# Order of work in the choice of experts and in the first rope: a two-layer kernel of attention and experts on one core

## What is computed

```python
x = x + tanh(g_xattn[0]) * xattn0(layernorm(x), ctx, ...)   # 16 heads; queries and context rows with rope
x = x + tanh(g_ffn[0])   * ffn0(layernorm(x), ...)          # 8 experts, top 2
x = x + tanh(g_xattn[1]) * xattn1(layernorm(x), ctx, ...)   # 16 heads; rope on the context alone
x = x + tanh(g_ffn[1])   * ffn1(layernorm(x), ...)          # 16 experts, top 2, and a shared expert
...
# ffn1
logits = xt @ Wr.T + bias
topk_val, topk_idx = top_k(softmax(logits), 2)
w = topk_val / (sum(topk_val) + 1e-9)
y = einsum('tei,eih->teh', silu(xt @ Wg) * (xt @ Wu), Wd)   # only the two chosen experts of a token count
routed = einsum('tke,tk,teh->th', one_hot(topk_idx), w, y)
shared = (silu(xt @ sWg) * (xt @ sWu)) @ sWd
return routed + shared
```

## Time and profile before

| what | value |
|---|---|
| median of 3 runs | 529.0 us (528.54 to 530.12) |
| profiled execution | 532.13 us |
| its span, first to last instruction | 530.3 us |
| PE busy | 469.5 us (89%) |
| DVE busy | 385.2 us (73%) |
| ACT busy | 197.5 us (37%) |
| POOL busy | 172.4 us (33%) |
| mean granted TensorE clock | 0.939 |

### The profile page before, as it was taken

One profiled execution on the slowest core, in us unless ns is written; L12 is line 12 of the kernel. 1 busy time (PEld: TensorE's weight loads), 2 busy tenths in 40 slices (PEclk: granted clock), 3 DMA queues, 4 the chain that ended last, 5 costly groups with the idle time before them and its releaser, 6 DMA issues.

```text
span 530.3 us, 9094 instructions
## 1 busy us (share of the span) xinstructions
PE 469.5 (89%) x3172; PEld 390.8 (74%) x3172; DVE 385.2 (73%) x847; ACT 197.5 (37%) x376; POOL 172.4 (33%) x150
## 2 busy tenths in 40 slices
PE   4699999999999999998999899999999976899700
PEld 4468667667765799887889788887799865899600
DVE  6979889889889865789777848677855585666323
ACT  3224233132151531433332356654662501466400
POOL 4825101101104000364551023532273306564064
PEclk9899999999999899999999999999799777999955
DMA  8302202211420300002100534322312303369344
GB/s 271 119 1 79 80 3 77 79 37 42 138 77 1 136 2 1 0 1 61 37 24 1 202 96 135 105 74 90 119 61 91 100 1 83 95 171 143 110 123 131
DMA packets 20286, 42.42 MB, mean 80 GB/s; under 512 B 3392, under 2 KB 10816, under 8 KB 20256
## 3 DMA queue, kind: packets, MB, share of 16 engines
q1 hardware_dynamic: 18000, 35.85, 20.3%
q0 software_dynamic: 2256, 6.16, 5.7%
HBM read 35.85 MB, written 6.16 MB: 79 GB/s over the span
## 4 chain that ended last, share of the span: by engine, by line
PE 63%; DVE 16%; issue 9%; POOL 6%; DMA 3%; ACT 1%; POOLq 0%; SPq 0%; DVEq 0%
PE ps L581 12%; PE ps L582 12%; PE ps L583 12%; PE ps L733 8%; PE ps L629 3%; POOL fg L564 2%; PE ps L681 2%; PE ps L589 2%; POOL probs L448 2%; PE ps L639 1%; DMA xg<-xn_rows,idx 1%; POOL experts_split L470 1%; PE ps L602 1%; PE ps L996 1%; DVE rstd L1488 1%
## 5 line engine op out<-in xcount | busy, mean ns | idle before, releaser
L448 POOL TENSOR_TENSOR probs<-probs,rowrec 128x512 f32<-128x512 f32 x28 | 28.7, 1045 | 160.3 <-DVE rowrec L1547 160.0
L1103 ACT ACTIVATE PT_hi<-ps 128x512 fp32r<-128x512 f32 (+1 forms) x64 | 35.5, 600 | 55.8 <-PE ps L639 52.4
L581 PE MATMUL ps<-xs_hi,A_hi 128*128 128x512 f32 x128 | 52.4, 409 | 1.5 <-DVE xs_lo L1501 1.5
L583 PE MATMUL ps<-xs_hi,A_lo 128*128 128x512 f32 x128 | 50.5, 395 | 0.0
L582 PE MATMUL ps<-xs_lo,A_hi 128*128 128x512 f32 x128 | 50.4, 394 | 0.0
L1510 DVE TENSOR_TENSOR PT_lo<-ps,PT_hi 128x512 fp32r<-128x512 f32 (+1 forms) x64 | 41.4, 686 | 7.7 <-ACT PT_hi L1103 7.3
L470 POOL TENSOR_TENSOR experts_split<-experts_raw,experts_split 128x768 fp32r<-128x768 f32 (+1 forms) x16 | 29.2, 1843 | 26.6 <-ACT experts_split L1103 26.6
L556 POOL DMA_INDIRECT xg<-xn_rows,idx x31 | 30.1, 970 | 21.2 <-PE ps L996 11.5
L581 PE MATMUL ps<-N_hi,PT_hi 128*128 128x256 f32 x128 | 36.4, 284 | 0.0
L582 PE MATMUL ps<-N_lo,PT_hi 128*128 128x256 f32 x128 | 36.1, 282 | 0.0
L583 PE MATMUL ps<-N_hi,PT_lo 128*128 128x256 f32 x128 | 36.0, 281 | 0.0
(11 more groups left out here) (224 smaller groups left out, 1333.5 us busy)
## 6 DMA issues: line engine op xcount, KB each, us to landing
W<-attn SPq DMA_DIRECT2D x8, 704.0 KB, 4.1
W<-attn SPq DMA_DIRECT2D x8, 672.0 KB, 4.4
W<-attn SPq DMA_DIRECT2D x16, 320.0 KB, 4.3
y_rows<-yout SPq DMA_DIRECT2D x15, 256.0 KB, 3.1
WF<-ffn SPq DMA_DIRECT2D x8, 384.0 KB, 4.2
experts_raw<-ffn SPq DMA_DIRECT2D x2, 1536.0 KB, 6.8
experts_raw<-ffn SPq DMA_DIRECT2D x2, 1152.0 KB, 5.6
X<-x SPq DMA_DIRECT2D x4, 256.0 KB, 4.9
```

Source lines behind the costliest of these rows:

```text
L448: nc.gpsimd.tensor_tensor(part, part, rowrec[:, 4 * h:4 * h + 4, :].unsqueeze(3).to_broadcast([P, 4, 2, L]), ALU.mult).then_inc(s.p, 1)
L581: nc.tensor.matmul(dst, lhs[0], rhs[0], start=start, stop=False)
L583: return nc.tensor.matmul(dst, lhs[1], rhs[0], start=False, stop=stop)
L1103: return nc.scalar.activation(dst, src, ACT.Copy)
```

## The change

- GpSimd's rope waits until VectorE has normalised its last tile of the first norm.
- ScalarE splits all three experts of the last weight group ahead of the transposed tiles of the last norm, instead of one there and two behind.
- In `sparse_ffn` TensorE does the first half's sums between the second router and `ranks`, and the shared expert's second half between `positions` and `slot_tokens`. The bridges change: three ahead of the transposes go, fifteen ahead of `ranks` become five ahead of the sums, ten come ahead of `slot_tokens`. Block transposes use banks 6 and 7, block results banks 2 and 3.
- The one-hot rows are four operations of 4x128 columns on float32 and integer inputs instead of sixteen of 128 on bf16; two conversions for them go.
- The token numbers are made by ScalarE (eight small scaled copies) instead of GpSimd.
- VectorE adds the shared sums of tiles 0 and 1 ahead of the second half's lower part, and makes the chosen experts' weights in the block loop.

```diff
                 pool.wait_ge(context_cols_loaded, 16 * 4)
+
+                pool.wait_ge(ln[0].xn, ln[0].before + 4)
                 step(kvT_s, kvT_s, for_batches(cosT_s[:], NB), ALU.mult)
...
-        SHARED_OUT = (6, 7, 4, 7)
+        SHARED_OUT = (2, 3, 4, 3)
...
-                pool.wait_ge(s.table, 16)
-                pool.wait_ge(s.routed_dve, BLOCK)
-                for k in range(2):
-                    tok = table[:, TTOK:TTOK + NT].unsqueeze(2).to_broadcast([P, NT, NCOL])
-                    nc.gpsimd.tensor_tensor(btok[:, k * NT:(k + 1) * NT, 0, :], beq[:, k * NT:(k + 1) * NT, :], tok,
-                                            ALU.mult).then_inc(s.btok, 1)
...
                 router(0)
-                bridge(3, 5)
                 transpose_tiles(3, 1, (6, 7))
                 router(1).then_inc(s.routed_pe, 1)
-                bridge(15, 5)
+
+                bridge(5, 5)
+                shared_down(0)
+                shared_down(1)
                 ranks()
-                bridge(1, 2)
+                bridge(2, 0)
                 positions()
                 pe.wait_ge(l.lo, l.before + 4)
-                shared_down(0)
-                shared_down(1)
+                shared_gate_up(1)
+                bridge(10, 6)
                 slot_tokens()
-                shared_gate_up(1)
                 pe.wait_ge(s.routed_dve, EXPERTS_OF)
...
                 act.wait_ge(s.w[4], 16)
-                expert_upper(13)
+                for e in range(*WGROUPS[4]):
+                    expert_upper(e)
                 transposed_tiles(3, 0, (0, 1))
...
-                expert_upper(14)
-                expert_upper(15)
                 shared_gates(0)
...
+
                 nc.scalar.activation(btok[:, :, 1, :], beq[:], ACT.Identity,
-                                     scale=table[:, TTOK + NT:TTOK + NT + 1]).then_inc(s.btok_act, 1)
+                                     scale=table[:, TTOK + NT:TTOK + NT + 1]).then_inc(s.btok, 1)
+                of_tile = [v.rearrange("p (k t) b -> p k t b", k=2) for v in (btok[:, :, 0, :], beq[:])]
+                for t in range(NT):
+                    op = nc.scalar.activation(of_tile[0][:, :, t], of_tile[1][:, :, t], ACT.Copy, scale=float(P * t))
+                op.then_inc(s.btok, 1)
...
-                link(V.tensor_copy(offsf[:], offs[:]))
-                dve.wait_ge(s.masks, 1)
-                for q in range(2 * NT):
-                    op = V.tensor_scalar(onehot[:, q, :], iota_bf[:], offsf[:, q:q + 1], None, ALU.is_equal)
-                    if q % 4 == 3:
-                        op.then_inc(s.onehot, 1)
+                for q in range(4):
+                    at_ = slice(4 * q, 4 * q + 4)
+                    V.tensor_tensor(onehot[:, at_, :], table[:, TIOTA:TIOTA + P].unsqueeze(1).to_broadcast([P, 4, P]),
+                                    offs[:, at_].unsqueeze(2).to_broadcast([P, 4, P]),
+                                    ALU.is_equal).then_inc(s.onehot, 1)
...
                 shared_hidden(1)
+                shared_add(0)
+                shared_add(1)
                 dve.wait_ge(s.hhi, 2)
                 V.tensor_tensor(hT1[1][:, HALF:2 * HALF], hid1[:, 1, :], hT1[0][:, HALF:2 * HALF].bitcast(F32),
                                 ALU.subtract).then_inc(s.h, 1)
-                for t in range(4):
-                    shared_add(t)
-
-                dve.wait_ge(s.exp, 2)
-                link(V.tensor_reduce(mx[4][:], lz[:], AX, ALU.add))
...
+                shared_add(2)
+                shared_add(3)
...
                         for t in range(4, NT):
                             shared_add(t)
+                    elif i == 2:
+                        choice_weights()
```

More of the change, by code:

```diff
@@ L180, in build @@
         posf, idxf = at_word("posf", [P, 2 * NT], RC + 336), at_word("idxf", [P, NCOL], RC + 352)
-        offsf, iota_bf = at_word("offsf", [P, 2 * NT], RC + 384), at_word("iota_bf", [P, P], RC + 400, BF16)
         ecmp = at_word("ecmp", [P, NCOL, E1], FR + RE)
@@ L251, in __init__ @@
                 s.whi, s.wlo, s.whole = sem(p + "whi"), sem(p + "wlo"), sem(p + "whole")
-                s.btok_act = sem(p + "btok_act")
                 s.xn = [sem(f"{p}xn{k}") for k in range(2)]
@@ L978, in slot_tokens @@
                     pe.wait_ge(s.btok, 2)
-                    pe.wait_ge(s.btok_act, 1)
                     for q in range(2 * NT):
@@ L995, in block_transposes @@
                         for c in range(NCH):
-                            last = nc.tensor.transpose(psum[2 + i % 2][:, b * DM + c * P:b * DM + (c + 1) * P],
+                            last = nc.tensor.transpose(psum[6 + i % 2][:, b * DM + c * P:b * DM + (c + 1) * P],
                                                        xg[:, (first_of(i) + b) % XG, c * P:(c + 1) * P], ident[:])
@@ L1037, in block_down @@
                     for b in range(width(i)):
-                        out_ = psum[6 + i % 2][:, b * DM:(b + 1) * DM]
+                        out_ = psum[2 + i % 2][:, b * DM:(b + 1) * DM]
                         hi, lo = (part[:, i % 2, b * INTER:(b + 1) * INTER] for part in hTb)
@@ L1065, in sparse_ffn @@
                 pe.wait_ge(s.wlo, E1 + 1)
-                bridge(4, 2)
+                bridge(4, 6)
                 block_transposes(0)
@@ L1359, in rows_upper @@
                     n = width(i) * DM
-                    copy(xT[0][:, i % 2, 0:n], psum[2 + i % 2][:, 0:n]).then_inc(s.bxhi, 1)
+                    copy(xT[0][:, i % 2, 0:n], psum[6 + i % 2][:, 0:n]).then_inc(s.bxhi, 1)
                 def block_gates(i):
@@ L1382, in block_rows @@
                     n = width(i) * DM
-                    copy(yout[:, i % YB, 0:n], psum[6 + i % 2][:, 0:n]).then_inc(s.by, 1)
+                    copy(yout[:, i % YB, 0:n], psum[2 + i % 2][:, 0:n]).then_inc(s.by, 1)
                 def whole(t, bank):
@@ L1412, in sparse_ffn @@
                 copy(ones_bf[:], table[:, TONE:TONE + P])
-                copy(iota_bf[:], table[:, TIOTA:TIOTA + P])
                 copy(before_bf[:], table[:, TU:TU + P]).then_inc(s.masks, 1)
@@ L1861, in sparse_ffn @@
                 shared_hidden(1)
-                dve.wait_ge(s.hhi, 2)
-                V.tensor_tensor(hT1[1][:, HALF:2 * HALF], hid1[:, 1, :], hT1[0][:, HALF:2 * HALF].bitcast(F32),
-                                ALU.subtract).then_inc(s.h, 1)
                 def shared_add(t):
@@ L1869, in shared_add, with choice_weights @@
                                            tgate[:, 3:4], X[:, t, :], ALU.mult, ALU.add).then_inc(s.x, 1)
-                for t in range(4):
-                    shared_add(t)
-                dve.wait_ge(s.exp, 2)
-                link(V.tensor_reduce(mx[4][:], lz[:], AX, ALU.add))
[L1876 to L1880, removed]
+                shared_add(0)
+                shared_add(1)
+                dve.wait_ge(s.hhi, 2)
+                V.tensor_tensor(hT1[1][:, HALF:2 * HALF], hid1[:, 1, :], hT1[0][:, HALF:2 * HALF].bitcast(F32),
+                                ALU.subtract).then_inc(s.h, 1)
+                shared_add(2)
+                shared_add(3)
+                def choice_weights():
+                    dve.wait_ge(s.exp, 2)
+                    link(V.tensor_reduce(mx[4][:], lz[:], AX, ALU.add))
+                    link(V.scalar_tensor_tensor(mx[4][:], mx[4][:], EPS_TOPK, mx[5][:], ALU.mult, ALU.add))
+                    link(V.tensor_scalar(mx[4][:], mx[4][:], 1.0, None, ALU.add))
+                    link(V.reciprocal(mx[4][:], mx[4][:]))
+                    link(V.tensor_scalar(cw[:, 0], mx[4][:], tgate[:, 3:4], None, ALU.mult))
+                    V.tensor_tensor(cw[:, 1], cw[:, 0], mx[5][:], ALU.mult)
                 def rows_lower(i):
@@ L1884, in rows_lower @@
                     n = width(i) * DM
-                    lower(xT[1][:, i % 2, 0:n], psum[2 + i % 2][:, 0:n], xT[0][:, i % 2, 0:n], s.bx)
+                    lower(xT[1][:, i % 2, 0:n], psum[6 + i % 2][:, 0:n], xT[0][:, i % 2, 0:n], s.bx)
                 def block_hidden(i):
```

## The result

The changed kernel took 515.4 us in the median of four runs (513.5 to 519.1), against 529.6 for the kernel before beside it: a ratio of 0.9717, 95% interval 0.967 to 0.9765. The profiled execution took 516.55 us.

What follows compares the result with a forecast made beforehand. TensorE's matmuls bound most of the kernel, VectorE two stretches: before attention 0 and the expert choice. Terms 6.9 + 2.5 + 0.6 + 0.3 + 3.8 - 0.5 = 13.6 gave 518.5 profiled, 515.4 us median; range 510.5 to 520.5.

Steps and rivals of the forecast that it cites:

- rope behind the norm: Norm ahead of attention 0: VectorE's stalls beside GpSimd's rope go, first scores move from 39.84 to 32.9, gain 6.9 us.
- split of 14 and 15, to the logits: Choice of experts: GpSimd's subtractions end ahead of the norm's links, second router's logits come 2.5 us earlier.
- ranks, to the packed places: Choice of experts, without the long bridge ahead of the ranks: gain between 0.2 and 1.0 us, taken as 0.6.
- one-hot rows and token numbers, to the index: Up to the token index: VectorE's rows get shorter but TensorE is now last, gain 0.3 us.
- index to the first block: From first gather's issue to first block: 6.85 us instead of 10.65, set by transposing the second landed block, gain 3.8.
- weights' links: first block to the end: Block loop: 1.4 us of links on VectorE where it has 0.85 idle, loss 0.5 us, between 0 and 1.4.
- slower rival: Rope beside VectorE's query rotation takes twice as long, scores begin 8.2 us later, kernel 1.5 slower at 530.5; chance 0.03.
- cover: Norm ahead of attention 0: something unseen holds the first scores, so the first 6.9 us go, 522.3; chance 0.05.
- The clock is lost in the choice: Choice of experts: TensorE rests before the ranks, its clock falls to half, time 518.5 to 520.2 us; chance 0.23.

Runs made afterwards that it cites:

- second profile: The changed kernel, unaltered, profiled again on the chip of two later kernels: span 514.70 us, median of its runs 516.0 us.
- old order: The changed kernel with four shared sums and the choice's weights again ahead of the first pair's low half on VectorE: 515.1 us, ratio 0.967.
- new order and no bridge: The changed kernel with VectorE's block loop reordered (weights and later shared sums moved) and the bridge of ten matmuls taken out: 511.1 us, ratio 0.9648.

## Why the prediction was right

The forecast was 515.4, the median 515.4. That they agree to the digit is luck. The span fell by 15.6 us where the sum had 13.6, and the median lay 1.15 below the profiled execution (516.55, forecast 518.5), not 3.1 as in the kernel before: two errors of 2.0 cancel. The four runs spread over 5.6 us, far more than the 1.6 that the prediction took as what a measurement can tell, and a second set of six has a median of 516.0. Both profiles are 15.6 shorter than before's, but not by the same steps, so the clock in attention 1 is not what made the 2.0. The prediction's own steps against the second profile, whose clock fell in attention 1 where before's did, and the first:

| step | forecast | second profile | first profile |
|---|---|---|---|
| rope behind the norm | 6.9 | 7.0 | 6.2 |
| split of 14 and 15, to the logits | 2.5 | 2.8 | 4.1 |
| ranks, to the packed places | 0.6 | 1.1 | 1.1 |
| one-hot rows and token numbers, to the index | 0.3 | 0.3 | 0.3 |
| index to the first block | 3.8 | 3.8 | 3.7 |
| weights' links: first block to the end | -0.5 | 0.5 | -1.6 |
| unchanged stretch up to the end of attention 1 | 0 | 0.1 | 1.8 |

**Rope.** Right in mechanism and size. The rope ran from 17.48 to 32.66, 15.2 us, as long as before, and is last: PE had ended its products at 32.0 and waited for G (33.43). In the first profile the two tiles ended 0.4 later than worked out, and the scores 0.5 later (33.43 against 32.9). The slower rival, a rope stalled in its turn, needed 28.8 us. The rope alone, put behind the norm in the kernel before, gave 7.16 at the scores, so the stall was not cover either.

**Split.** Right in mechanism. Both outcomes that I priced occur: at a clock that holds up to the logits the step is worth 4.1 (priced 4.2, in the first profile), at one that falls on the way 2.7 to 2.9. The late split in the changed kernel shows the same 4.1, of which the stall is 2.1, and that some 2 of it can come back from the first block on.

**Ranks.** Under-sized, 1.1 against 0.6. It was the upper bound that held: DVE's choice and lower halves end last, and PE is ready. The split alone brings it too.

**One-hot rows and token numbers.** Right, PE was last, by the bridge of ten: without it the index came 1.0 sooner. But the working had a wrong price in it: I read 0.22 us for an old row, which is 0.17 and, on two of the sixteen, POOL's stall, and so gave the new rows a credit that belongs to the token numbers' move. The reading of the Trainium skill's VectorE: DVE Perf Modes (Side-by-side) was at fault too: that section adds some 150 cycles of start to each instruction, which I had left out of the streaming. With it, an estimate from that page is 16 x 0.2 = 3.2 against 4 x 0.7 = 2.8, a gain of 0.4 instead of a loss of 1.6; the runs gave 2.70 with a cast of about 0.2 against 2.49. Either way the rows are hidden behind PE.

**Index to the first block.** Right in sum, and the landing of the second pair ends it, as worked out (6.85 forecast, 6.83 and 6.99). The sum's parts were not what I had them to be: the half's place and DVE's order are each enough for most of it (7.7 or 7.9 against 10.65), where the prediction credited them together.

**Weights' links in the block loop.** The third block's low half began directly behind the last of the weights (445.35 and 445.27 in the first profile). It came 3.40 and 3.41 behind the second's in the two profiles, against 3.03 in before and 3.06 with the old order: a loss of 0.4, forecast 0.5. But the clock at the first block moves this stretch by more, 1.4 between the two profiles (8.12 and 6.76).

**The rivals.** "The clock is lost in the choice" came about in part. The clock did fall there, to 0.54 and 0.53, but it was back (0.99 and 1.00) ahead of the second half and the bridge, so the index lost nothing; and the ranks, which the rival put at 0.3, gained 1.1 in both profiles. What I had not seen is that the clock falls once more behind the gathers' first issue. The exchange of PSUM banks, taken as free, was not tried alone.

## What to carry to other kernels

Look for DVE links of a few elements that take as long as a POOL operation beside them: they stand still for it, and moving POOL's work behind them is worth the whole stall if what POOL makes has slack. When two edits each shorten one stretch with two engines near its end, price them together and one by one: here either was enough. Judge a change of 1% by several runs set against their granted clock, and compare profiles stage by stage only where the clock fell at the same places.

## What the runs showed of the hardware that was not expected

- An unchanged stretch of some 370 us took 372.3, 370.6 or 367.3 us in profiles of these kernels, by how long TensorE's clock was at 0.50 in the value products of the two attentions: some 10 us in all in the changed kernel's second profile, some 7 in its first (from 176.5 to 179.9 and from 371.0 to 374.5), and none with the new order and no bridge. In attention 1 it fell behind a pause of 0.9 us ahead of a probability's transposes; the kernel in which it did not fall has the same pause. The Trainium skill's TensorE: Matmul & The Clock Gate (What's actually happening) states that the moment of the change differs from run to run of one kernel. The traces agree: in the choice the changed kernel's clock fell 8.0 us behind the last sum of attention 1 in one profile and 6.1 in the other.
- Gains don't add where the clock moves: 4.1 us in the choice, half of it a stall, left 1.9 us in the span in one pair of profiles, because the half clock at the first block lasted longer.
- The same links beside the same rope lost 6.9 us in one kernel and 8.9 in another, where the rope began 0.3 us sooner. The rope took 15.2 us in both, and as long with the links out of its way: DVE alone paid.
